# Norms begun in the block before: the head of a grouped attention and of a ternary MLP

## Chip, cores and metric

One core of one Trainium2 chip. The metric is the device time of one execution in microseconds, the median over several runs. In what follows TensorE is PE in the rows, VectorE is DVE, ScalarE is ACT, GpSimd is POOL.

## The reference

A decoder of four layers on x of shape (4, 256, 256), fp32. Each layer adds an attention, a cross attention and a feed-forward part, each on a layer norm of x:

```python
def _layernorm(x, axis=-1, eps=1e-05):
    m = jnp.mean(x, axis=axis, keepdims=True)
    v = jnp.var(x, axis=axis, keepdims=True)
    return (x - m) / jnp.sqrt(v + eps)
...
    x = x + _L1_ffn_ref(_layernorm(x, axis=-1), ...)
    x = x + _L2_attn_ref(_layernorm(x, axis=-1), L2_attn_wq, L2_attn_wk, L2_attn_wv, L2_attn_wo)
...
    x = x + _L3_xattn_ref(4, 256, 256, L3_xattn_w, L3_xattn_u, _layernorm(x, axis=-1), ctx_2048)
    x = x + _L3_ffn_ref(_layernorm(x, axis=-1), L3_ffn_W_up, L3_ffn_W_gate, L3_ffn_W_down)
```

Three parts matter here. `_L1_ffn_ref` is a mixture of 8 experts (top 2) with a narrow hidden size of 128, an up projection to 256 and a core product. `_L3_xattn_ref` is a recurrence over time (WKV) with keys from the norm and values from the context. `_L3_ffn_ref` is silu(x Wu') * (x Wg') Wd' with 1024 hidden columns and weights replaced by -1, 0 or 1 times a scale.

## The kernel before

The residual X lies in SBUF as 8 tiles of 128 tokens x 256, in four groups g of two tiles. The program is a row of blocks; within one, each engine has its own list of instructions, ordered by hand, with semaphores between them. At a block's end all engines meet in a barrier.

`norm_steps` (L273) gives the steps of a norm for one group. `measure` (VectorE): two statistics (L322), two aggregates (L325). `root` (ScalarE, L389): a square root, which needs a table of its own. `apply` (VectorE): a reciprocal (L329), two scalings (L332) into H. `turn` (TensorE): four transposes (L426) into a PSUM bank. `copy` (ScalarE): out of it, to HT (L394), or, where bf16 parts are wanted, to the first part (L396). Then `rest_of` (VectorE, L337) subtracts the first part, `second` (ScalarE, L400) rounds the rest, `third` (VectorE, L341) subtracts again: fp32 as a sum of three bf16 parts. `columns(g)` is the wait for the last of these. `warm` (L267) issues filler products of 512 columns, whose result is not used.

`experts1` (L2015) ends so: 42 pieces of up product, Gelu, gating and down product; the last down products; VectorE reads both PSUM banks (L2213) into MT; TensorE issues 8 up products (L2118) into banks 0 to 3, twice round; VectorE adds each to X (L2217). The next block, `project_paired` of layer 2 (L1225), runs the whole norm and the first projections: product and values (L1263, L1271) on TensorE, the rotation on VectorE (L1292 to L1296) and GpSimd (L1307), spread to masked copies on ScalarE (L1330).

`wkv_scan` (L2709) is the recurrence by scans. Its end: the last quotient (L2765), TensorE turns it onto X in PSUM (L2872, L2877), ScalarE copies the sum back to X (L2835), once for each of the four batches.

`ternary_mlp` (L2935) is the last block. It runs a norm with three parts from its first step on, then for 8 chunks i of the hidden columns and 2 halves c of the tokens: up and gate product (L2959, 12 matmuls), Silu (L2995), product with the gate (L3025), three parts (L3001, L3030, L3005, L3034), down product (L2969, 12 matmuls), with each up product one chunk ahead of the down product. At the end X gets the sum (L3049) and goes to DRAM.

TensorE's order at its head is

```python
                    warm(pe, 3, 8)
                    for g in range(TT // 2):
                        norm["turn"](pe, g)
                        warm(pe, 3, 4)
                    warm(pe, 3, 6)
                    for c in range(NCH):
                        go_up(0, c)
```

The first layer's `mlp` (L1532) is built alike, with groups 0 and 1 of its norm begun in the block before it, and turns only of groups 2 and 3 at its head.

## Time and profile before

| | |
|---|---|
| median of 3 runs | 1171.09 us (1167.62 to 1173.74) |
| the profiled execution | 1173.02 us |
| its span, first to last instruction | 1171.3 us |
| TensorE busy | 1058.0 us (90%) |
| VectorE busy | 778.7 us (66%) |
| ScalarE busy | 572.6 us (49%) |
| GpSimd busy | 384.9 us (33%) |
| mean granted TensorE clock | 0.968 of full |

The busy shares are averages over some thirty blocks with different limits; what a change in one place is worth is read in the timeline of that place. The profiled execution's time is its span and 1.7 us around it.

### The profile page before, as it was taken

The page shows a single profiled execution, that of the slowest core. Times are in us where ns is not written, and L with a number is a line of the kernel's source. Part 1 is how long each engine was busy: PE and PEld are TensorE (multiplying, and loading weights), DVE is VectorE, ACT ScalarE, POOL GpSimd, SP SyncE. Part 2 cuts the span into 40 slices and gives each one's busy share as a digit, 9 for nine tenths or more (in the row PEclk, how much of TensorE's full clock was granted, in tenths as well). Part 3 has the DMA queues.
Part 4 walks back from the last instruction along what each step waited for, and adds up shares of the span by engine and source line. Part 5 has one row for each costly group of instructions (what it writes and reads, how often), then busy time and mean ns, then how long its engine had stood idle before and what let it go on. Part 6 is the DMA issues. An engine that isn't in the chain of part 4 may idle for free. (4 is left out here: it accounts for less than half of the span.)

```text
span 1171.3 us, 22560 instructions
## 1 busy us (share of the span) xinstructions
PE 1058.0 (90%) x8162; PEld 657.3 (56%) x8177; DVE 778.7 (66%) x2357; ACT 572.6 (49%) x1193; POOL 384.9 (33%) x499
## 2 busy tenths in 40 slices
PE   5779989998989999899998989899999999867898
PEld 3447645567855554455665545467777555543455
DVE  6753468659668654567887678673454777969755
ACT  3859425564425624374555266516433154547443
POOL 2445403000001210033666425437776033843000
PEclk9889999998999999999999899999999999987999
DMA  9100000000031030000000000536665400000001
GB/s 376 59 1 3 1 1 2 1 1 2 1 157 79 2 144 1 0 1 3 2 3 2 1 2 2 194 109 206 187 193 151 144 1 2 2 1 0 1 1 37
DMA packets 23486, 60.74 MB, mean 52 GB/s; under 512 B 3681, under 2 KB 12009, under 8 KB 22480
## 3 DMA queue, kind: packets, MB, share of 16 engines
q1 hardware_dynamic: 18864, 48.92, 11.9%
q0 software_dynamic: 4512, 10.37, 3.0%
q8 instruction: 67, 1.10, 0.4%
q14 instruction: 43, 0.35, 0.1%
HBM read 52.95 MB, written 8.29 MB: 52 GB/s over the span
## 5 line engine op out<-in xcount | busy, mean ns | idle before, releaser
L977 ACT ACTIVATE PT<-PS 128x384 f32<-128x384 f32 (+1 forms) x320 | 153.2, 530 | 162.0 <-PE PS L721 115.9
L872 DVE CUSTOM_DVE_ANT_0 junk<-PS,TRI 128x128 bf16<-128x128 f32 (+1 forms) x384 | 111.0, 352 | 2.4 <-PE PS L702 2.4
L702 PE MATMUL PS<-KS,QM 32*128 32x128 f32 (+1 forms) x768 | 90.1, 344 | 8.7 <-ACT PT L977 1.6
L702 PEld LDWEIGHTS PS<-KS,QM 32*128 32x128 f32 x768 | 73.6, 184 | 41.2 <-issue 21.9
L270 PE MATMUL PS<-identb 128*128 128x512 bf16 x355 | 89.0, 390 | 3.7 <-PEq L481 1.1
L721 PE MATMUL PS<-QM,KS 32*128 32x256 f32 (+1 forms) x768 | 88.6, 348 | 0.5 <-ACT PT L977 0.2
L1058 POOL TENSOR_TENSOR OD<-OD 128x256 f32<-128x256 f32 x16 | 11.6, 728 | 226.7 <-DVE OD L932 226.7
L1036 POOL TENSOR_SCALAR_AFFINE_SELECT PT<-PT 128x512 f32<-128x512 f32 x96 | 60.4, 636 | 69.8 <-ACT PT L977 69.8
L791 PE MATMUL PS<-PT,VM 128*32 128x256 f32 (+1 forms) x1024 | 72.7, 359 | 8.5 <-POOL PT L1036 7.9
L1307 POOL TENSOR_TENSOR ROT<-RC,RS 128x512 f32<-128x512 f32 x16 | 20.3, 1270 | 148.6 <-DVE RS L1296 145.8
L721 PEld LDWEIGHTS PS<-QM,KS 32*128 32x128 f32 x768 | 65.8, 184 | 3.3 <-issue 2.7
L2393 PE MATMUL PS<-WU,XT 128*128 x188 | 63.6, 461 | 0.3 <-ACT XT L2487 0.3
L270 PEld LDWEIGHTS PS<-identb 128*128 128x128 bf16 x355 | 32.4, 99 | 46.2 <-issue 16.6
L2207 DVE SCALAR_TENSOR_TENSOR HB<-HA,ROW,GB 128x512 f32<-128x512 f32 x40 | 30.0, 751 | 39.6 <-ACT HA L2142 39.2
L2705 POOL DMA_INDIRECT chosen<-YB,DEST x47 | 48.1, 1022 | 18.8 <-issue 11.6
L2690 POOL DMA_INDIRECT XB<-token_rows,FROM x47 | 46.3, 985 | 20.7 <-issue 11.3
L2142 ACT ACTIVATE HA<-PS,VEC 128x512 f32<-128x512 f32 x42 | 28.7, 687 | 48.8 <-PE PS L2061 48.8
L2413 PE MATMUL PS<-WD,HIDT 128*128 128x256 f32 x188 | 48.2, 380 | 0.0
L426 PE MATMUL PS<-CST,H 128*128 128x128 f32 x128 | 23.3, 315 | 25.9 <-DVE H L332 25.6
L2553 DVE TENSOR_TENSOR HID<-PS,AE 128x176 f32<-128x176 f32 x47 | 16.0, 341 | 43.8 <-ACT AE L2493 43.7
L881 DVE TENSOR_REDUCE MA<-PS 128x4 f32<-128x1024 f32 x32 | 38.9, 1220 | 8.8 <-PE PS L702 7.6
L2061 PE MATMUL PS<-GH,WB 128*128 128x512 f32 x84 | 43.4, 599 | 0.6 <-ACT GH L2125 0.6
(399 smaller groups left out, 2649.2 us busy)
## 6 DMA issues: line engine op xcount, KB each, us to landing
WD<-w2d_in SPq DMA_DIRECT2D x47, 256.0 KB, 3.4
WU<-w2u_in SPq DMA_DIRECT2D x1, 5632.0 KB, 18.2
WA<-wl_in SPq DMA_DIRECT2D x1, 5137.0 KB, 16.1
GB<-gate_rows SPq DMA_DIRECT2D x8, 512.0 KB, 7.5
WU<-chosen SPq DMA_DIRECT2D x16, 256.0 KB, 5.7
WB<-wb_in SPq DMA_DIRECT2D x1, 3208.0 KB, 19.2
WA<-wa_in SPq DMA_DIRECT2D x1, 2560.0 KB, 16.0
WA<-w2s_in SPq DMA_DIRECT2D x6, 384.0 KB, 17.0
```

The lines of the kernel that those rows point to most:

```text
L270: pe.matmul(PS[:, bank, :].rearrange("p (a n) -> p a n", a=4), identb[:], identb[:].rearrange("p (a n) -> p a n", a=1).to_broadcast([P, 4, ...
L702: return pe.matmul(PS[:, s, m * T:m * T + n], queries(U, v)[rows, m * P:(m + 1) * P], keys(U, v)[rows, 0:n], start=True, stop=True, skip_g ...
L721: last = pe.matmul(bank, keys(U, v)[rows, n * P:(n + 1) * P], queries(U, v)[rows, lo:hi], start=n == 0, stop=r > 1, skip_group_check=True, ...
L791: last = pe.matmul(PS[at:at + 32, 7, side + lo:side + hi], VM[:, U % 2, n, h * P + at:h * P + at + 32], PT[:, g % 3, s, n * T:n * T + hi - ...
L872: last = dve.tensor_tensor_reduce(junk[:, s, m * P:m * T + P], PS[:, s, m * T:m * T + (m + 1) * P], TRI[:, (1 - m) * P:T], 1.0, NEG, ALU.a ...
L977: act.activation(PT[:, g % 3, st_slot(k), 0:W], PS[:, st_bank(g, k), 0:W], ACT.Exp, scale=scale).then_inc(S["at_exp"], 1)
L1036: pool.affine_select(v, v, [[0, 4], [1, P]], ALU.is_ge, 0.0, base=0, channel_multiplier=-1).then_inc(S["at_masked"], 1)
L2061: pe.matmul(PS[:, n % 2, :], w, GH[:, c * CH:(c + 1) * CH], start=True, stop=True).then_inc(S["up_ps"], 1)
L2393: last = pe.matmul(up_bank(b), XT[:, b % 2, k * P:(k + 1) * P], mine[:, k * 2 * I2:(k + 1) * 2 * I2], start=k == 0, stop=k == KD - 1)
L2413: last = pe.matmul(down_bank(b), HIDT[:, b % 2, k * P:(k + 1) * P], WD[:, b % RINGW, k * D:(k + 1) * D], start=k == 0, stop=k == 1)
L2690: pool.indirect_dma_start(XB[:, j, :], None, token_rows, bass.IndirectOffsetOnAxis(FROM[:, b:b + 1], 0)).then_inc(S[f"x_slot{j}"], 16)
L2705: pool.indirect_dma_start(chosen, bass.IndirectOffsetOnAxis(DEST[:, b:b + 1], 0), YB[:, b % RINGE, :], None, bounds_check=SPARE_ROW - 1, o ...
```

## The change

- The first norm of layer 2 is begun in `experts1`: VectorE measures and applies groups 0 and 1 there between the additions, ScalarE roots and copies them, TensorE turns them. The sum is read in two halves, and the last up products go to six banks instead of four. `project_paired` does only groups 2 and 3.
- The norm of the ternary MLP is begun in `wkv_scan`: measures and roots of groups 0 and 1 at the end of VectorE's and ScalarE's lists. `parts` moves to another place in SBUF's order of allocation.
- In `ternary_mlp` VectorE's and ScalarE's lists at the head are written out in a new order, with a Silu on one element ahead of the copies 2 and 3 (it brings the table) and the first Silu ahead of `second(3)`. TensorE's head is as before. The last chunk's down products go part by part.

```diff
@@ def experts1(norm, following):
+            following["begin"]()
+            last_bank = lambda t: PS[:, (0, 1, 2, 3, 6, 7, 0, 1)[t], 0:D]
...
-                    pe.wait_ge(S["dve_mark"], d["dve_mark"] + 3)
+                    pe.wait_ge(S["x_added"], d["x_added"] + TT // 2)
                     for t in range(TT):
-                        if t >= 4:
-                            pe.wait_ge(S["x_added"], d["x_added"] + TT // 2 + t - 3)
-                        pe.matmul(PS[:, t % 4, 0:D], MT[:, t * P:(t + 1) * P], wB("up"), start=True, stop=True
+                        if t % TPC == 0:
+                            pe.wait_ge(S["dve_mark"], d["dve_mark"] + 3 + t // TPC)
+                        if t >= 6:
+                            pe.wait_ge(S["x_added"], d["x_added"] + TT // 2 + t - 5)
+                        pe.matmul(last_bank(t), MT[:, t * P:(t + 1) * P], wB("up"), start=True, stop=True
                                   ).then_inc(S["o_proj"], 1)
+                    pe.wait_ge(S["x_added"], d["x_added"] + TT // 2 + 4)
+                    warm(pe, 2, 4)
+                    for g in range(BEGUN):
+                        following["turn"](pe, g)
+                        warm(pe, 2, 4)
...
+                    for g in range(BEGUN):
+                        following["root"](act, g)
+                    for g in range(BEGUN):
+                        following["copy"](act, g)
...
+                    for c in range(NCH):
+                        dve.wait_ge(S["down_ps"], d["down_ps"] + NWK - NCH + c + 1)
+                        dve.tensor_scalar(MT[:, c * CH:(c + 1) * CH], PS[:, 4 + c, :], cc[:, 2:3], None, ALU.add
+                                          ).then_inc(S["dve_mark"], 1)
+                    for g in range(BEGUN):
+                        add_last(2 * g)
+                        add_last(2 * g + 1)
+                        dve.wait_ge(S["x_added"], d["x_added"] + TT // 2 + 2 * g + 2)
+                        following["measure"](dve, g)
+                    for g in range(BEGUN):
+                        following["apply"](dve, g)
+                    for t in range(2 * BEGUN, TT):
+                        add_last(t)
@@ def wkv_scan(left, norm, following):
                     quotients(B - 1)
+                    for g in range(BEGUN):
+                        dve.wait_ge(S["x_added"], d["x_added"] + g + 1)
+                        following["measure"](dve, g)
...
                     for b in range(1, B):
                         copy(b)
+                    for g in range(BEGUN):
+                        following["root"](act, g)
@@ def ternary_mlp(exact, SC, norm):
+                    def last_down(c):
+                        for j, name in enumerate(("pr_first", "pr_second", "pr_third")):
+                            pe.wait_ge(S[name], d[name] + NCH * (n - 1) + c + 1)
+                            for q in range(TPC):
+                                last = down_step(n - 1, c, q, j)
+                        last.then_inc(S["down_ps"], 1)
...
-                    norm["scalar"](act)
...
+                    norm["copy"](act, 0)
+                    norm["copy"](act, 1)
+                    norm["second"](act, 0)
+                    norm["root"](act, 2)
+                    norm["second"](act, 1)
+                    norm["root"](act, 3)
+                    act.activation(AO[:, 0, 0:1], SC[:, 0:1], ACT.Silu)
+                    norm["copy"](act, 2)
+                    norm["copy"](act, 3)
+                    norm["second"](act, 2)
                     silu(*work[0])
+                    norm["second"](act, 3)
...
-                    norm["vector"](dve)
+                    for g in range(BEGUN):
+                        norm["apply"](dve, g)
+                    norm["measure"](dve, 2)
+                    norm["rest_of"](dve, 0)
+                    norm["rest_of"](dve, 1)
+                    norm["third"](dve, 0)
+                    norm["measure"](dve, 3)
+                    norm["third"](dve, 1)
+                    norm["apply"](dve, 2)
+                    norm["apply"](dve, 3)
+                    for g in (2, 3):
+                        norm["rest_of"](dve, g)
+                    for g in (2, 3):
+                        norm["third"](dve, g)
```

VectorE at the end of `experts1`, in the changed program (L2235 reads the sum, L2231 is an addition to X, L322 to L332 are the norm's):

```order
L2235 TENSOR_SCALAR MT<-PS,cc 128x512 [waits down_ps] x2
L2231 TENSOR_TENSOR X<-X,PS 128x256 [waits o_proj] x2
L322 BN_STATS HEAD_STATS<-X 128x6 [waits x_added]
L322 BN_STATS HEAD_STATS<-X 128x6
L325 BN_AGGR HEAD_MOM<-HEAD_STATS 128x2 [waits stats] x2
L2231 TENSOR_TENSOR X<-X,PS 128x256 [waits o_proj] x2
L322 BN_STATS HEAD_STATS<-X 128x6 [waits x_added]
L322 BN_STATS HEAD_STATS<-X 128x6
L325 BN_AGGR HEAD_MOM<-HEAD_STATS 128x2 [waits stats] x2
L329 RECIPROCAL HEAD_RSTD<-HEAD_STD 128x2 [waits std]
L332 TENSOR_SCALAR H<-X,HEAD_MOM,HEAD_RSTD 128x256 [waits rstd]
L332 TENSOR_SCALAR H<-X,HEAD_MOM,HEAD_RSTD 128x256
```

Before, the reading was one instruction and the eight additions stood in one piece, with the block's end behind them; the norm's rows stood in the next block.

ScalarE from the last copies of the recurrence into the ternary MLP, before and now (L2835 and L2865 are the copies of X, L389 the root, L396 the first part, L400 the second part, L2995 and L3035 the Silu):

```order
L2835 ACTIVATE X<-PS 128x512 [waits turned] x3
L2727 UNCONDITIONAL_BRANCH
L2987 UNCONDITIONAL_BRANCH [waits barrier_Pool_Activation_PE_DVE_SP_release]
L389 ACT_TABLE_LOAD
L389 ACTIVATE std<-mom,CST 128x2 [waits moments] x3
L396 ACTIVATE parts<-PS 128x2x256 [waits turned]
L389 ACTIVATE std<-mom,CST 128x2 [waits moments]
```

```order
L2865 ACTIVATE X<-PS 128x512 [waits turned] x3
L389 ACT_TABLE_LOAD
L389 ACTIVATE HEAD_STD<-HEAD_MOM,CST 128x2 [waits moments] x2
L2754 UNCONDITIONAL_BRANCH
L3029 UNCONDITIONAL_BRANCH [waits barrier_Pool_Activation_PE_DVE_SP_release]
L396 ACTIVATE parts<-PS 128x2x256 [waits turned] x2
L400 ACTIVATE parts<-HT 128x2x256 [waits part_rest]
L389 ACTIVATE HEAD_STD<-HEAD_MOM,CST 128x2 [waits moments]
...
L400 ACTIVATE parts<-HT 128x2x256 [waits part_rest]
L3035 ACTIVATE AO<-PS,SC 128x512 [waits up_ps]
L400 ACTIVATE parts<-HT 128x2x256 [waits part_rest]
```

The table load and two roots moved from behind the branch, which is the block's end, to ahead of it; the first Silu stands ahead of the last L400.

VectorE at the head of the ternary MLP, in the changed program:

```order
L322 BN_STATS HEAD_STATS<-X 128x6 x2
L325 BN_AGGR HEAD_MOM<-HEAD_STATS 128x2 [waits stats] x2
L337 TENSOR_TENSOR HT<-PS,parts 128x2x256 [waits part_first] x2
L341 TENSOR_TENSOR parts<-HT,parts 128x2x256 [waits part_second]
L322 BN_STATS HEAD_STATS<-X 128x6 x2
L325 BN_AGGR HEAD_MOM<-HEAD_STATS 128x2 [waits stats] x2
L341 TENSOR_TENSOR parts<-HT,parts 128x2x256 [waits part_second]
L329 RECIPROCAL HEAD_RSTD<-HEAD_STD 128x2 [waits std]
L332 TENSOR_SCALAR H<-X,HEAD_MOM,HEAD_RSTD 128x256 [waits rstd]
L332 TENSOR_SCALAR H<-X,HEAD_MOM,HEAD_RSTD 128x256
```

Before, `measure` and `apply` of all four groups (L322 to L332) stood ahead of the first L341; now the scalings of groups 2 and 3 stand behind the L341 of groups 0 and 1, while TensorE's list still has its turns of groups 2 and 3 ahead of the first up product.

## Rows read from the trace of the kernel before

**Rows 1.** Chain of waits that ended last: start us, us, what.
```profile
1102.90 7.72 PE PS L2959 x35
...
1158.73 2.60 PE PS L2959 x12
...
1161.35 0.70 ACT AO L2995
```

**Rows 2.** Timeline, end of the experts: start us, us, engine, line, what [idle before it <- releaser].
```profile
485.24 2.85 PE L2067 MATMUL PS<-HB,WB 128*128 128x512 f32 x6
...
489.47 3.72 PE L2118 MATMUL PS<-WB,MT 128*128 128x256 f32 x16 [1.38 <-DVE MT L2213]
490.21 3.44 DVE L2217 TENSOR_TENSOR X<-X,PS 128x256 f32<-128x256 f32 x8 [0.79 <-PE PS L2118]
...
500.06 1.98 PE L1263 MATMUL PS<-HT,WA 128*128 128x512 f32 x4 [0.39 <-ACT HT L394]
...
502.09 0.73 DVE L1292 STREAM_SHUFFLE RS<-PS 128x512 f32<-128x512 f32 x1
...
504.13 1.26 POOL L1307 TENSOR_TENSOR ROT<-RC,RS 128x512 f32<-128x512 f32 x1 [90.31 <-DVE RS L1296]
...
507.16 2.55 ACT L1330 ACTIVATE QM<-ROT,CST 128x512 f32<-128x512 f32 x4
```

**Rows 3.** Timeline, end of the recurrence and head of the ternary MLP.
```profile
1089.66 0.69 DVE L2765 TENSOR_TENSOR EV<-PS,EV 128x512 f32<-128x512 f32 x1
...
1091.60 0.60 ACT L2835 ACTIVATE X<-PS 128x512 f32<-128x512 f32 x1 [2.30 <-PE PS L2877]
1092.45 1.28 ACT L389 ACT_TABLE_LOAD   x1 [0.26 <-PEq L2727]
...
1092.49 1.89 PE L270 MATMUL PS<-identb 128*128 128x512 bf16 x8 [0.93 <-PEq L2727]
...
1093.75 0.29 ACT L389 ACTIVATE std<-mom,CST 128x2 f32<-128x2 f32 x1
...
1094.23 0.13 DVE L329 RECIPROCAL rstd<-std 128x2 f32<-128x2 f32 x1
...
1110.45 1.47 PE L2969 MATMUL PS<-WA,MP 128*128 128x256 bf16 x12
```

**Rows 4.** Groups by line, 1092.4 to 1103.6 us: xcount | busy us, mean ns | idle.
```profile
L322 DVE BATCH_NORM_STATS2 stats<-X 128x6 f32<-128x256 f32 x8 | 3.0, 412 | 2.1 <-PEq L2727 2.1
L332 DVE TENSOR_SCALAR H<-X,mom,rstd 128x256 f32<-128x256 f32 x8 | 2.9, 410 | 0.1
...
L337 DVE TENSOR_TENSOR HT<-PS,parts 128x512 f32<-128x512 f32 x4 | 2.7, 683 | 0.0
L426 PE MATMUL PS<-CST,H 128*128 128x128 f32 x16 | 2.6, 287 | 1.2 <-DVE H L332 1.2
L400 ACT ACTIVATE parts<-HT 128x512 bf16<-128x512 f32 x4 | 2.5, 626 | 0.8 <-DVE HT L337 0.8
L396 ACT ACTIVATE parts<-PS 128x512 bf16<-128x512 f32 x4 | 2.3, 587 | 1.1 <-PE PS L426 1.1
```

**Rows 5.** Windows: length, PE, PEld, DVE, ACT, POOL busy (instructions), granted clock, DMA share, GB/s.
```profile
1072.60:1075.29 2.69, 0.01 (x1) 0.00 (x1) 2.69 (x6) 2.65 (x7) 0.00 (x0) 0.92 0.00 0
1075.29:1078.00 2.71, 2.71 (x3) 1.17 (x4) 2.71 (x1) 2.71 (x8) 2.63 (x3) 0.50 0.00 0
...
674.48:676.73 2.25, 0.00 (x1) 0.03 (x1) 1.55 (x3) 2.22 (x4) 0.00 (x0) 1.00 0.00 0
676.73:678.73 2.00, 2.00 (x20) 1.05 (x20) 0.83 (x1) 1.16 (x3) 0.00 (x0) 1.00 0.00 0
1047.60:1064.40 16.80, 7.52 (x17) 4.00 (x18) 15.60 (x31) 14.64 (x32) 1.40 (x1) 0.50 0.00 0
```

**Rows 6.** Timeline, head of the first layer's MLP.
```profile
216.62 0.69 ACT L1622 ACTIVATE AO<-PS,VEC 128x512 f32<-128x512 f32 x1 [0.83 <-PE PS L1553]
...
218.60 0.98 PEld L1553 LDWEIGHTS PS<-QT,WA 128*128 128x128 bf16 x6 [0.94 <-DVE QT L341]
```

**Rows 7.** Timeline, the last products and additions.
```profile
1165.52 1.40 DVE L3049 SCALAR_TENSOR_TENSOR X<-PS,SC,X 128x512 f32<-128x512 f32 x2
...
1165.65 1.48 PE L2969 MATMUL PS<-WA,MP 128*128 128x256 bf16 x12 [0.69 <-DVE MP L3034]
...
1167.18 1.41 DVE L3049 SCALAR_TENSOR_TENSOR X<-PS,SC,X 128x512 f32<-128x512 f32 x2 [0.26 <-PE PS L2969]
```

More of the change, by code:

```diff
@@ L432, in tensor @@
                 turn(pe, g)
-        return dict(rest_of=rest_of, parts=parts, vector_rest=vector_rest, scalar_rest=scalar_rest, begin=begin, root=root, copy=copy, measure=measure, apply=apply, vector=vector, scalar=scalar, tensor=tensor, product=product, turn=turn, columns=columns, tokens=tokens)
+        return dict(rest_of=rest_of, third=third, second=second, parts=parts, vector_rest=vector_rest, scalar_rest=scalar_rest, begin=begin, root=root, copy=copy, measure=measure, apply=apply, vector=vector, scalar=scalar, tensor=tensor, product=product, turn=turn, columns=columns, tokens=tokens)
     def add_sums(gate=None):
@@ L2012, in mixing, with experts1 @@
             done["moments"] += 3 * TT
-    def experts1(norm):
+    def experts1(norm, following):
         E = E1
@@ L2720, in wkv_scan @@
             done["dve_chain"] += 5
+            done["turned"] += B
+            done["x_added"] += B
+            following["begin"]()
             K = HT[:].rearrange("p k (b t) -> p k b t", t=T)
@@ L2886, in _ @@
                     turn(B - 1)
-            done["turned"] += B
-        left.close()
     def ternary():
@@ L2945, in ternary_mlp @@
             MP = tmp("MP3", [P, 3, NCH, CH], BF16)
-            norm = norm_steps(st, X, H, to_HT, parts=parts, tbank=lambda g: 4 + g)
+            parts = norm["parts"]
             d = dict(done)
@@ L2980, in _ @@
                         go_up(0, c)
-                    for i in range(n):
+                    for i in range(n - 1):
                         for c in range(NCH):
-                            if i + 1 < n:
-                                go_up(i + 1, c)
+                            go_up(i + 1, c)
                             go_down(i, c)
+                    for c in range(NCH):
+                        last_down(c)
                 @block.scalar
                 def _(act):
-                    norm["scalar"](act)
                     def silu(i, c):
@@ L3104, in layers @@
         cross_attention(32, gamma=rv("gamma"), loads=late_loads, following=following)
-        experts1(following)
+        first = norm_steps(None, X, H, to_HT, tbank=lambda g: 4 + g, begun=False)
+        experts1(following, first)
         wb_store.close()
@@ L3114, in layers @@
                                   "v": wL("v3", KD), "o": wL("o3", KD)}, 16, 0.25, turned=True, begun=second)
-        wkv_scan(left, norm)
-        parts = sb("parts", [P, 3, KD, B * T], BF16)
-        ternary_mlp(exact, SC, parts)
+        parts = left.enter_context(nc.sbuf_tensor("parts", [P, 3, KD, B * T], BF16))
+        last = norm_steps(None, X, H, to_HT, parts=parts, tbank=lambda g: 4 + g, begun=False)
+        wkv_scan(left, norm, last)
+        ternary_mlp(exact, SC, last)
+        left.close()
     layers()
```

34 lines of the change are left out of this document (17 added, 17 removed).

## The prediction

> **What bounds the kernel now.** The chain of waits says where the end is set: from 1102.9 us to 1161 us it is TensorE alone, the ternary MLP's up and down products back to back [rows 1]. What moves their start moves the end of the program by the same amount. So I read the timeline at the three places that the change touches: the end of the first expert stage [rows 2], the end of the recurrence and the head of the ternary MLP [rows 3], and the last products [rows 7]. The groups by line give the norm steps' durations [rows 4]. The first layer's MLP, whose order is copied, shows how that order behaves [rows 6], and the windows show TensorE's granted clock around its pauses [rows 5]. At all three places work is serial: TensorE waits for a norm, and nothing else fills the time.
>
> **Place 1, end of the experts to the first projection.** Before: the last down products end at 488.09, TensorE stands for 1.38 us until VectorE has read both halves of the sum in one step, the eight up products run from 489.47, eight additions from 490.21 take 3.44 us, and the next block's first projection starts at 500.06 [rows 2]. Now:
> - The sum is read in two halves. The first is complete before the last down product's end and hides beside it, so the up products start at about 488.0. The second half, some 0.7 us (half of the 1.38), is done by 488.8, before the fifth product asks for it.
> - VectorE: two additions from 488.75 (0.43 each), measure of group 0 (two statistics and two aggregates; two measures lie between 1092.49 and 1094.23 [rows 3], so 0.88 us), two additions, measure of group 1, apply 0, apply 1 (two scalings of 0.41 us each [rows 4], the reciprocal ahead in their overlap: 0.82), and four additions. 488.75 + 4 x 0.43 + 2 x 0.88 + 2 x 0.82 + 4 x 0.43, with 0.1 us of waits on its own results, is 495.7.
> - TensorE turns group 0 when it is applied, at 493.2, and group 1 after four filler products of 0.22 us, at 494.6; the last four fillers are out at 495.95. ScalarE has been idle since the last Gelu, so the table load for the root hides there.
> - With 0.3 us between blocks the first projection starts at 496.3 instead of 500.06: **-3.8 us**. VectorE still has measures and applies 2 and 3 ahead of the first rotation (496.35 + 2 x 0.88 + 2 x 0.82 = 499.75), which before began at 502.09: 2.3 us earlier rather than 3.8, so 1.5 us are missing. The cover is ScalarE's order: it copies groups 2 and 3 before the first values and the first spread, which before began at 507.16, 1.77 us after GpSimd's sum of the rotation was ready (504.13 + 1.26) [rows 2]. 1.5 is less than 1.77, so the spread still comes 3.8 us earlier and the gain passes on; if that cover were gone, 1.5 us would be given back. The projection now carries the wait for the late weights that the fillers carried; those were issued without standing, so it costs nothing.
>
> **Place 2, recurrence to ternary MLP.** The measures of groups 0 and 1 go behind the last quotient on VectorE, which ends at 1090.35, so they are over by 1092.1 and cost nothing. But the two roots stand behind ScalarE's last copy of X, which ends at 1092.20, and need another table: a load of 1.28 us and two roots of 0.29 us, 1094.0, and all engines wait for it in the block's barrier. The new block starts at 1094.3 instead of 1092.5 [rows 3]. Before, the first reciprocal ran at 1094.23 [rows 3]; so beginning the norm early gains nothing for group 0.
>
> From 1094.3 on, with the new order on VectorE and ScalarE and the same one on TensorE (all four turns stand ahead of the first up product):
> - TensorE's eight fillers end at 1096.03, later than group 0 is applied (1095.24). Turn 0 at 1096.03, turn 1 behind it and four fillers at 1097.38, ending 1098.04 (four transposes, 0.66 us from the first start to the last end: 0.29 of [rows 4] for one, three issues of 0.12).
> - VectorE: applies 0 and 1, measure 2, rest 0 and 1 (each behind ScalarE's 0.59 us copy), third 0, measure 3, third 1, over at 1101.5, each tensor step 0.68 us. Only then apply 2, done at 1102.3, and apply 3 at 1103.1.
> - TensorE, idle from 1098.7, turns group 2 at 1102.34, group 3 at 1103.70, issues ten fillers and starts the first up product at 1106.35, against 1102.90 [rows 1]: +3.5 us.
> - The second half's up product needs third 3. ScalarE now takes the first Silu (0.70 us [rows 1], behind the first up product's end at 1108.94) ahead of second 3 (0.63), and third 3 (0.68) follows [rows 4]: 1110.95. TensorE stands for 2.0 us. The first layer's MLP shows just this: a Gelu at 216.62, its next up product only at 218.60 [rows 6]. Before, that product started right behind the first.
> - Two up products of 2.6 us later [rows 1], the first down product starts at 1116.13; before it was 1110.45 [rows 3]. That is **+5.7 us**, and everything behind is bound by TensorE, so it stays.
>
> **TensorE's clock at place 2.** TensorE now rests twice: from its last turn's end, just before ScalarE's copy of 1091.60 [rows 3], to 1094.3 (2.7 us), and from 1098.7 to 1102.34 (3.6 us). In the row of 1072.60, a pause of 2.69 us from the full 2.4 GHz, the granted clock falls (its mean over the pause is 0.92), and it is 0.50 (1.2 GHz) all through the next 2.71 us: with the pause's end over 3 us at half clock, I take 3.3 [rows 5]. Of five such pauses of 2.69 to 2.87 us in this trace at full clock all five are followed by half clock; one of 2.25 us is not [rows 5]. While TensorE is the one that is waited for, a stretch of 3.3 us at half clock does half its work: 1.7 us lost. Unknown is how much of each stretch falls on work that matters. The lower bound is 0 (the 2.25 us row); the upper is three such stretches, about 5 us, as the level may stay low: it did for 16.8 us from 1047.6, where TensorE was busy for 7.52 [rows 5]. I take two stretches, **+3.4 us**, since both pauses are at or over the length that always fell.
>
> **Place 3, the end.** The last piece's products are issued part by part, so only four products of 0.12 us (1.48 / 12 [rows 7]) wait for the last third, at 1165.65: TensorE would end near 1166.2 instead of 1167.13. But VectorE's first two additions run until 1166.92 anyway, and its idle time before the third was 0.26 us [rows 7]. So **-0.3 us**; the other 0.7 us hide behind VectorE.
>
> **Sum:** -3.8 + 5.7 + 3.4 - 0.3 = **+5.0 us**. The profiled execution took 1173.02 us, 1.7 us more than its span and 1.9 us more than the median of the three runs, 1171.09. That one would become 1178.0; the median, which I predict, **1176.1 us**. A measurement of this kernel can tell 0.5% from no change, 5.9 us; the forecast is just under it.
>
> **A rule against the sum.** The roots' table load costs 1.28 us in the trace: the load of 1092.45 ends at 1093.73 and the root stands at 1093.75, with nothing between [rows 3]. The Trainium skill, "ScalarE: Activation LUTs", section "What ACT_TABLE_LOAD costs", adds a drain of about 1380 ns to every switch. By that the block would start about 1.4 us later, and the sum would be an estimated +6.4 us. The trace has the load alone, so I keep 1.28 and give the drain the small chance below.
>
> **Rivals.**
> - *The clock holds.* A pause that shares its time with much activity around it may pass, as at 674.48. Then the sum is -3.8 + 5.7 - 0.3 = +1.6 us, 1172.7. For it: fillers surround both pauses. Against: five of five. 0.15.
> - *The low clock stays longer, slower than before.* Mechanism: with half clock already at 1094.3 the eight fillers take 3.5 us, both turns and with them copy, rest and third of groups 0 and 1 come 1.7 to 2.5 us later, the pause behind them follows at half clock, and the 2.0 us wait for the first Silu meets it while it is still low, and it stays low beyond. It decides once the clock is down before the first filler. Price: +5.7 + 5 or more, so the sum is +7 to +9: 1178 to 1180. For it: the long low stretch from 1047.6. 0.24.
> - *ScalarE stands some more than its load at the recurrence's end,* 1.4 us, before the barrier lets the block begin. The same load at a block's head shows nothing of the kind [rows 3]. +6.4, 1177.5: 0.03.
> - *Place 1 gives nothing*, because VectorE's later rotation or a lost cover takes its gain: -3.8 becomes -1: +7.8, 1178.9. 0.05.
> - *Faster.* Stretches at half clock lie elsewhere too, and all stages behind place 1 move by 3.8 us, which may shorten or lengthen them. The one from 1047.6 to 1064.4 held 7.5 us of TensorE work [rows 5]; at full clock that is 3.8 us less. With that, and the clock holding at place 2, it is -2; to be faster by 5.9 a second such one must vanish. 0.08.
> - *Forecast as it stands,* +2.5 to +7: 0.45.
>
> **How the numbers follow.** Of the forecast's 0.45, some 0.32 lie under 5.9 us and 0.13 over. Within 0.5%: 0.32 + 0.15 = 0.47, and 0.01 from place 1. Slower: 0.13 + 0.24 + 0.03 + 0.04 = 0.44. Faster: 0.08. The range for 8 in 10 goes from below the case in which the clock holds, 1170.5, to the longer low clock, 1181; the forecast's own is 1173.6 to 1178.1.
>
> **What would show it.** Right: the first projection starts 3.8 us after the place where the down products end plus 4.5 us, that is some 8.3 us behind them instead of 12; a table load with two roots between ScalarE's last copy of the recurrence and the new block; turn 2 waiting some 3.6 us for the apply; the second up product waiting about 2 us behind a Silu; the granted clock at 0.5 around there. Wrong: if from the last quotient to the first ternary down product it is not at least 25 us (before: 1110.45 - 1090.35 = 20.1), the step on the order at place 2 falls; if it is about 26 with the clock at 1.0, only the clock's term falls.

## Result and the profile after

| | before | after |
|---|---|---|
| median, 10 executions each | 1172.09 us (1167.44 to 1175.90) | 1177.24 us (1171.85 to 1181.85) |
| the profiled execution | 1173.02 us | 1176.54 us |
| its span | 1171.3 us | 1174.8 us |
| mean granted TensorE clock in it | 0.968 | 0.966 |

The ratio is 1.0046, with [1.0028, 1.0064] as its 95% interval: by it the change is 5.4 us slower (3.3 to 7.5); the two medians differ by 5.15 us. The forecast was +5.0. The two profiled executions differ by 3.5 us. The difference between these two numbers is a question of its own, and the experiments come to it.

**Place 1.** Timeline of the changed kernel, from the last down products of the experts into the next block: start us, us, engine, line, what [idle before it <- releaser].

```profile
484.80 2.85 PE L2073 MATMUL PS<-HB,WB 128*128 128x512 f32 x6
...
485.71 1.28 ACT L389 ACT_TABLE_LOAD   x1
...
487.62 3.69 PE L2126 MATMUL PS<-WB,MT 128*128 128x256 f32 x16
487.69 0.75 DVE L2235 TENSOR_SCALAR MT<-PS,cc 128x512 f32<-128x512 f32 x1 [0.23 <-PE PS L2073]
...
492.70 0.66 PE L426 MATMUL PS<-CST,H 128*128 128x128 f32 x4 [0.53 <-DVE H L332]
...
495.96 1.96 PE L1263 MATMUL PS<-HT,WA 128*128 128x512 f32 x4 [0.45 <-PEq L2048]
...
499.22 0.73 DVE L1292 STREAM_SHUFFLE RS<-PS 128x512 f32<-128x512 f32 x1
...
501.27 1.28 POOL L1307 TENSOR_TENSOR ROT<-RC,RS 128x512 f32<-128x512 f32 x1 [87.89 <-DVE RS L1296]
...
503.03 2.55 ACT L1330 ACTIVATE QM<-ROT,CST 128x512 f32<-128x512 f32 x4
```

The down products end at 484.80 + 2.85 = 487.65. The up products start at that moment, without the pause of 1.38 us [rows 2], and the first projection starts 8.31 us behind the end, not 11.97 (500.06 - 488.09 [rows 2]): -3.66 us. The table load at 485.71 lies beside the down products. The program is 0.44 us ahead already before this place (487.65 against 488.09), which is not the change's. Net of it, VectorE's rotation starts 2.43 us earlier, and the spread (L1330) 3.69 us earlier. So the gain passes on whole, although VectorE's share of it is smaller.

**Place 2.** Timeline of the changed kernel, same columns, from the last quotient to the first ternary down product.

```profile
1085.94 0.69 DVE L2792 TENSOR_TENSOR EV<-PS,EV 128x512 f32<-128x512 f32 x1
...
1086.68 1.16 PE L2910 MATMUL PS<-CST,EV 128*128 128x128 f32 x8 [0.88 <-DVE EV L2792]
...
1087.88 0.60 ACT L2865 ACTIVATE X<-PS 128x512 f32<-128x512 f32 x1 [2.31 <-PE PS L2910]
...
1088.49 1.28 ACT L389 ACT_TABLE_LOAD   x1
1089.79 0.48 ACT L389 ACTIVATE HEAD_STD<-HEAD_MOM,CST 128x2 f32<-128x2 f32 x2
...
1090.58 2.66 PE L270 MATMUL PS<-identb 128*128 128x512 bf16 x8 [2.73 <-PEq L2754]
...
1093.03 1.06 PE L426 MATMUL PS<-CST,H 128*128 128x128 f32 x4
...
1100.19 0.66 PE L426 MATMUL PS<-CST,H 128*128 128x128 f32 x4 [3.45 <-DVE H L332]
...
1104.14 2.75 PE L2990 MATMUL PS<-parts,WA 128*128 128x512 bf16 x12
1106.94 0.69 ACT L3035 ACTIVATE AO<-PS,SC 128x512 f32<-128x512 f32 x1 [3.63 <-PE PS L2990]
1107.52 0.62 ACT L400 ACTIVATE parts<-HT 128x512 bf16<-128x512 f32 x1
...
1108.92 5.35 PE L2990 MATMUL PS<-parts,WA 128*128 128x512 bf16 x24 [2.02 <-DVE parts L341]
...
1114.11 1.47 PE L3011 MATMUL PS<-WA,MP 128*128 128x256 bf16 x12
```

From the last quotient's start to the first down product it was 1110.45 - 1089.66 = 20.79 us [rows 3]; it is 1114.11 - 1085.94 = 28.17: +7.38 us. Each wait that the order promised is there: 2.73 us of TensorE behind the table load and the roots, 3.45 us for the applied group 2, and 2.02 us for the last part, which stands behind the Silu.

The chain of waits of the changed kernel says why the second wait is there: start us, us, what.

```profile
1096.55 0.69 DVE HT L337
1097.23 0.60 DVE parts L341
1097.84 0.66 DVE HEAD_STATS L322 x2
1098.50 0.22 DVE HEAD_MOM L325 x2
1098.71 0.57 DVE parts L341
1099.29 0.09 DVE HEAD_RSTD L329
...
1099.40 0.75 DVE H L332 x2
```

It runs through VectorE without a hole: the third parts of groups 0 and 1 (L341) and a measure stand ahead of group 2's apply (L332). The two L341 are parts for an up product that TensorE's list does not let run before turns 2 and 3.

TensorE's clock in windows of the changed kernel, around its pauses: length, PE, PEld, DVE, ACT, POOL busy (instructions), granted clock, DMA share, GB/s.

```profile
1087.84:1090.58 2.74, 0.01 (x1) 0.04 (x2) 0.52 (x4) 2.36 (x4) 0.00 (x0) 1.00 0.00 0
...
1091.60:1095.00 3.40, 3.40 (x11) 1.75 (x10) 1.86 (x7) 0.60 (x1) 0.00 (x0) 0.51 0.00 0
...
1096.74:1100.19 3.45, 0.00 (x1) 0.00 (x0) 3.41 (x11) 2.52 (x5) 0.00 (x0) 1.00 0.00 0
1100.20:1103.60 3.40, 3.40 (x20) 2.12 (x21) 2.22 (x6) 2.06 (x5) 0.00 (x0) 1.00 0.03 5
```

The pause behind the recurrence was followed by half clock (1.2 GHz): the eight fillers took 2.66 us instead of 1.89 [rows 3], and turn 0 took 1.06 instead of 0.66. The longer pause of 3.45 us was not; here the clock stayed at 2.4 GHz. The three other traces with this head (`e2`, `e4` and `e11` below) show the same: half clock behind the first pause, full clock behind the second.

**Place 3.** Timeline of the changed kernel, its last products and additions, same columns as above.

```profile
1168.59 1.34 PE L3011 MATMUL PS<-WA,MP 128*128 128x256 bf16 x8 [0.40 <-ACT MP L3045]
1169.18 2.72 DVE L3113 SCALAR_TENSOR_TENSOR X<-PS,SC,X 128x512 f32<-128x512 f32 x4
```

The four additions run through where there was a hole of 0.26 us between them [rows 7]. From the first down product to the last addition's end it is 57.79 us instead of 58.14: -0.35.

The three add up to -3.66 + 7.38 - 0.35 = +3.4 us for the profiled execution, which is its difference of 3.5.

### The profile page after: what moved, and what is told of

The parts are those of the page before. It is cut to its first block and busy times, and to the rows that moved or that the text cites. A ratio compares the mean times of both kernels' runs of the same rounds, so it can differ in the third digit from the quotient of the medians.

```text
span 1174.8 us, 22573 instructions
## 1 busy us (share of the span) xinstructions
PE 1059.0 (90%) x8174; PEld 658.2 (56%) x8174; DVE 778.6 (66%) x2358; ACT 572.7 (49%) x1194; POOL 384.5 (33%) x499
## 5 line engine op out<-in xcount | busy, mean ns | idle before, releaser
L2714 POOL DMA_INDIRECT XB<-token_rows,FROM x47 | 46.0, 980 | 20.7 <-issue 10.7
L426 PE MATMUL PS<-CST,H 128*128 128x128 f32 x128 | 23.5, 317 | 27.7 <-DVE H L332 27.5
L2990 PE MATMUL PS<-parts,WA 128*128 128x512 bf16 x192 | 43.9, 379 | 2.0 <-DVE parts L341 2.0
```

The costliest lines, as they stand in the source:

```text
L2714: pool.indirect_dma_start(XB[:, j, :], None, token_rows, bass.IndirectOffsetOnAxis(FROM[:, b:b + 1], 0)).then_inc(S[f"x_slot{j}"], 16)
L2990: last = pe.matmul(PS[:, 2 * c + half, :], w[:, k, i * P:(i + 1) * P], parts[:, j, k, c * CH:(c + 1) * CH], start=k == 0 and j == 0, stop= ...
```

## Experiments

Twelve runs were made in three groups of four, each group on a chip of its own beside the kernel before: `e1` to `e4` (before: median 1199.93 us), `e5` and `e7` to `e9` (1201.76), `e6` and `e10` to `e12` (1175.01). They are eleven programs, the change itself among them; one was run twice. "Q" below is the start of the recurrence's last quotient, and "to down" the time from there to the first ternary down product: 20.79 us before, 28.17 in the change. On the first two of these chips the whole program takes some 25 us longer than on the third, nearly all of it in the second expert stage between places 1 and 2, where nothing was changed; the stretches at the three places are the same to 0.1 us. So the stretches are compared across chips, and the times only as ratios.

### Which part costs: the parts alone

`e1_place1_alone` has the change's `experts1` and `project_paired`, and the recurrence and `ternary_mlp` of before. `e2_places23_alone` is the reverse:

```diff
-        first = norm_steps(None, X, H, to_HT, tbank=lambda g: 4 + g, begun=False)
-        experts1(following, first)
+        experts1(following)
```

> Place 1 alone (the norm of layer 2 begun in the experts' tail), recurrence and ternary MLP as before. My theory: the first projection starts about 8 us behind the last down product instead of 12, and the last quotient of the recurrence is reached 3.7 us earlier; nothing after it changes, so the kernel is 3.7 us faster than before, ratio 0.997. Rival (the gain is given back on the way, or by stretches at half clock that fall elsewhere): the ratio is 1.000 or above.

Measured: ratio 0.9977 [0.9956, 0.9997]; the first projection 8.31 us behind the down products, to down 20.79. The rival's 1.000 lies just outside the interval.

> Places 2 and 3 alone, the experts as before. My theory: from the start of the last quotient (20.8 us before the first down product of the ternary MLP in the kernel before) it takes 26.5 us with the clock up and 28.2 with one stretch at half clock; the end gives 0.35 back; so +6 to +8 us, ratio 1.005 to 1.007. Rival (the loss comes from how the two parts meet, for instance the clock's phase that place 1 shifts): less than +4 us.

Measured: 1.0053 [1.0033, 1.0073]; 11.97 us to the first projection, to down 28.17. The stretches are additive to the hundredth: place 1 gains 3.66 us, place 2 loses 7.38, and neither changes the other.

### The clock: filling the pauses

`e3_pause_filled` puts twelve fillers behind the recurrence's last turn, for the first pause:

```diff
+                    warm(pe, 0, 12)
```

> The changed kernel with 12 filler products behind TensorE's last turn of the recurrence, which fill the 2.7 us pause until the new block. Clock theory: the granted clock stays at 1.0 at the head of the ternary MLP, the first turn ends 0.9 us or more earlier, and from the last quotient's start to the first down product it takes 26.5 us instead of 28.2. Rival (order and barrier alone cost the 7.4 us, and half clock hides beside the waits for VectorE): still 28 us. A second risk: the fillers end late and delay the block's start; 12 x 0.216 = 2.6 us from 1087.8 is just inside the pause.

Measured: 1.0021 [1.0004, 1.0038]; to down 30.01. TensorE's timeline in this run:

```profile
1114.46 2.75 PE L270 MATMUL PS<-identb 128*128 128x512 bf16 x12
1117.51 1.89 PE L270 MATMUL PS<-identb 128*128 128x512 bf16 x8 [0.30 <-PEq L2754]
...
1125.45 0.65 PE L426 MATMUL PS<-CST,H 128*128 128x128 f32 x4 [3.45 <-DVE H L332]
1125.94 1.42 PE L270 MATMUL PS<-identb 128*128 128x512 bf16 x4
...
1135.86 7.04 PE L2991 MATMUL PS<-parts,WA 128*128 128x512 bf16 x24 [2.02 <-DVE parts L341]
```

The first pause is gone, and the eight fillers take 1.89 us again. But now the clock fell in the second pause and once more behind the third, where 24 up matmuls took 7.04 us instead of 5.35. Turn 0 ended about 1 us earlier, as expected, but 30.01 is neither the theory's 26.5 nor the rival's 28: in this execution the fall came where it cost more. The second risk that was named came true in small: the fillers end late, and the block begins at Q + 4.79 instead of Q + 4.64.

`e9_both_pauses_filled` has those twelve and nineteen fillers behind turn 1:

```diff
-                        warm(pe, 3, 4)
+                        warm(pe, 3, 19 if g == 1 else 4)
```

> The changed kernel with 12 fillers behind the recurrence's last turn and 19 instead of 4 behind turn 1, so that TensorE works through both pauses. Clock theory: granted clock 1.0 up to the first up product, which starts 16.7 us behind the last quotient (18.2 in the changed kernel, 18.4 with the first pause alone filled), and the first down product at 26.5 us. Only the 2.0 us pause behind the first up product can still lower it. Rival (half clock is not what these 1.7 us are): 28 us.

Measured: 1.0032 [1.0011, 1.0053]; to down 26.64, and the window shows the full clock all through the head (same columns as the windows above):

```profile
1115.00:1139.40 24.40, 21.81 (x107) 10.47 (x107) 13.41 (x35) 11.77 (x21) 0.00 (x0) 1.00 0.00 1
```

So with the clock up place 2, new order and table load together, costs 26.64 - 20.79 = +5.85 us. What the clock took in the profiled execution of the change is 28.17 - 26.64 = 1.53 us, and in the run with one pause filled 30.01 - 26.64 = 3.37. Here too the twelve fillers put the block 0.15 us late (Q + 4.79), and turn 2 comes as much later, 7.94 us behind the block's start. Without that the price is an estimated +5.70 and the clock's part 1.68; the figures below use 5.85 and 1.53. The rival that half clock is not what these 1.7 us are falls (28 us), and so does the idea that the clock explains most of place 2.

### The order: taking back one step at a time

`e4_silu_behind_second` moves the first Silu behind the spread of group 3:

```diff
-                    silu(*work[0])
                     norm["second"](act, 3)
+                    silu(*work[0])
```

> The changed kernel with the first Silu put back behind second(3) on ScalarE. My theory: the 2.0 us in which TensorE stood before the second up product vanish, the two first up products run back to back, and from the last quotient's start to the first down product it takes 26.2 us (28.2 less 2.0). Rival (the Silu ahead saves as much later as it costs, as the first down product's chain starts from it): 27.5 us or more.

Measured: 1.0018 [0.9998, 1.0038]; to down 25.97 instead of 28.17. The two up products run as one group again, 7.93 us without a hole. The Silu's place is worth 2.2 us of the 5.85; the rival (27.5 us or more) falls.

`e5_table_early` loads the root's table ahead of ScalarE's last copy of X, by a root of a constant that nothing reads:

```diff
+                        if b == B - 1:
+                            act.activation(nsq[:], cst("eps"), ACT.Sqrt)
```

> The changed kernel with one square root on a single element ahead of ScalarE's last copy of X in the recurrence, so that the table is loaded in ScalarE's idle time. My theory: the load was on the path to the barrier; the new block's first filler starts 3.35 us behind the last quotient's start instead of 4.64, TensorE's pause there falls from 2.7 to 1.4 us, and the first down product comes 25.2 us behind the last quotient with the clock up (28.2 in the changed kernel), 26.9 or more if the clock falls in the second pause. Rival (the copy of X cannot run with the square root's table and another load follows, or the measures on VectorE set the block's end): 27.8 us or more.

Measured: 1.0050 [1.0017, 1.0082], 7 executions; to down 28.44. ScalarE and TensorE in its timeline:

```profile
1113.62 1.28 ACT L2881 ACT_TABLE_LOAD   x1
...
1114.91 0.20 ACT L2881 ACTIVATE nsq<-CST 128x1 f32<-128x1 f32 x1
...
1116.14 0.47 ACT L389 ACTIVATE HEAD_STD<-HEAD_MOM,CST 128x2 f32<-128x2 f32 x2
1116.92 1.89 PE L270 MATMUL PS<-identb 128*128 128x512 bf16 x8 [1.31 <-PEq L2755]
```

The block begins 1116.92 - 1113.71 = 3.21 us behind Q instead of 1090.58 - 1085.94 = 4.64: the load's 1.43 us are gone from the path. The last copy of X (1115.65 to 1116.25) and the two roots follow without a second load. But the clock fell behind the second pause and again behind the third as in `e3_pause_filled` (24 up matmuls took 7.04 us), so the gain does not show in the end: 28.44 lies in the range of the rival, but neither of the rival's two reasons is in the trace.

`e6_up_first` lets TensorE issue the first half's up product ahead of turns 2 and 3 and drops six fillers:

```diff
-                    warm(pe, 3, 6)
-                    for c in range(NCH):
-                        go_up(0, c)
+                        if g == 1:
+                            go_up(0, 0)
+                    go_up(0, 1)
```

> Edit, from the change: the first half of unit 0's up product stands ahead of the projections of tiles 2 and 3, the second half behind them, and the six fillers between go. Theory A (the second pause in the head is the time in which the first half's product and everything behind it could run, and the order of TensorE keeps them out): first up product at about 12 us behind the last quotient's start (18.20 in the change), the second half still waits for tiles 2 and 3, first down product at about 24.8 with the clock up (28.17 in the change), so about 3.4 us less than the change: ratio 1.000. Rival B (the parts of the second half bound the head alone): first up product early, but first down product at 27 or later and less than 1.2 us gained: ratio 1.002 to 1.005. Rival C: the clock falls behind the wait for tiles 2 and 3, which would put 1.5 to 3.4 us back on A, first down product at 26.3 to 28.2.

Measured: 0.9992 [0.9969, 1.0014]; first up product at Q + 13.65, to down 26.14. The clock was at half from 1087.4 to 1091.0, on the same eight fillers as in the change. So against the change's 28.17 TensorE's list alone was worth 2.0 us; the six fillers that were dropped had no part in it, since TensorE stood for 2.17 us behind the last filler even so. Theory A's 24.8 and its first up product at 12 are for the clock up. The stretch at half clock is the change's own (turn 1 starts at Q + 9.35, there Q + 9.34, with both pauses filled Q + 7.82 with the fillers' 0.15 in it). With its estimated 1.68 us taken off, 26.14 becomes 24.5 and 13.65 becomes 12.0: theory A holds, and of its 3.4 us against the change 2.0 are order and the rest is clock. Rival B (27 us or more) falls. Rival C's condition, a fall behind the wait for groups 2 and 3, did not come.

### Can the early norms pay

`e8_head_mended` combines the early table, TensorE's up product between the turns and the Silu behind the spread; it also moves `third(1)` ahead of `measure(3)` and has other numbers of fillers:

```diff
                     norm["turn"](pe, 1)
+                    warm(pe, 3, 9)
+                    go_up(0, 0)
                     norm["turn"](pe, 2)
...
+                        act.activation(nsq[:], cst("eps"), ACT.Sqrt)
...
-                    silu(*work[0])
                     norm["second"](act, 3)
+                    silu(*work[0])
```

> The changed kernel with place 2 mended: table loaded early, the first up product ahead of turns 2 and 3 and in their pause, thirds 0 and 1 ahead of measure 3, first Silu behind second(3), fillers 5, 2, 9 and 8. My theory: no pause of TensorE over 1.5 us but at the barrier, granted clock 1.0, first down product 20.7 us behind the last quotient's start, as in the kernel before (20.8): beginning the norm early is worth nothing there even when its costs are taken away, since ScalarE's copy and the barrier take the place of the first measures. Ratio 0.9965. Rival (the early measures were a gain that the order alone spoilt): 19.5 us or less.

Measured: 0.9986 [0.9965, 1.0007]; first up product at Q + 10.47, to down 22.04. That is 1.3 us over the expected 20.7, since the clock fell here, behind a pause of only 1.31 us:

```profile
1122.18 2.06 PE L270 MATMUL PS<-identb 128*128 128x512 bf16 x5 [1.31 <-PEq L2755]
1124.03 1.06 PE L426 MATMUL PS<-CST,H 128*128 128x128 f32 x4
```

`e10_interleaved`, the next kernel, has the same list on TensorE up to this point and the same pause of 1.31 us, and there the clock did not fall:

```profile
1089.27 1.24 PE L270 MATMUL PS<-identb 128*128 128x512 bf16 x5 [1.31 <-PEq L2755]
1090.35 0.60 PE L426 MATMUL PS<-CST,H 128*128 128x128 f32 x4
```

It puts the turns, copies, rests, spreads and parts of the four groups in the order in which they come ready, with the early table. ScalarE's list, for example:

```diff
+                    norm["root"](act, 2)
                     norm["copy"](act, 0)
                     norm["copy"](act, 1)
-                    norm["second"](act, 0)
-                    norm["root"](act, 2)
-                    norm["second"](act, 1)
                     norm["root"](act, 3)
-                    act.activation(AO[:, 0, 0:1], SC[:, 0:1], ACT.Silu)
+                    norm["second"](act, 0)
                     norm["copy"](act, 2)
+                    norm["second"](act, 1)
```

> Edit, from the change: the square root's table is loaded ahead of the recurrence's last output copy (as in the run with the early table), TensorE's projections of the four tiles stand in the order in which their parts come (five fillers, tile 0, two, tile 1, three, tile 2, three, tile 3, three, then both halves of the up product), ScalarE and VectorE alternate between the tiles in the same order, and the Silu of unit 0 goes behind the spread of tile 3. Theory A (what lengthened the head is the order and the table load, each of which can be taken back while the two norms stay ahead): first ternary down product 19.2 us behind the start of the last quotient (20.79 before, 28.17 in the change, 22.04 in the mended head), first up product at 11.4; with places 1 and 3 the sum is -3.7 -0.35 -1.6 = -5.6 us, ratio 0.995. Rival B (a stretch at half clock falls into it, as it did in the mended head at 22.04): 1.5 to 3.4 us more, first down product at 20.7 to 22.6, ratio 0.997 to 0.998. Rival C (beginning the norms early gives nothing that the order of before does not give): first down product at 20.8 or later with the clock up, and the time that of places 1 and 3 alone, 0.9947 to 0.997.

Measured: 0.9951 [0.9927, 0.9975]; first up product at Q + 12.59, to down 20.14, with one stretch at half clock while TensorE turned groups 2 and 3:

```profile
1095.00:1098.40 3.40, 3.34 (x11) 1.46 (x10) 2.73 (x7) 1.95 (x4) 0.00 (x0) 0.52 0.02 5
```

That is 0.65 us under the order of before even so: rival C, that nothing is to be gained on the order of before, is refuted in the trace, and B's mechanism probably took part of the 1.6 us. That the 0.65 us come from the early norms, and not from the new order and the fewer fillers, is not shown: an interleaved order without early norms was not run.

`e7_places13` keeps places 1 and 3 and leaves place 2 as it was, and `e12_places13_again` is the same program. Added to place 1 alone is only the end:

```diff
-                    for i in range(n):
+                    for i in range(n - 1):
...
+                    for c in range(NCH):
+                        last_down(c)
```

> Places 1 and 3 only: the norm of layer 2 begun in the experts' tail, the last down products part by part; recurrence and head of the ternary MLP as before. My theory: 8.3 us from the last down product of the experts to the projection, 20.8 us from the last quotient to the first down product, 57.8 us from there to the last addition: -3.7 and -0.35, ratio 0.9966 to before. Rival (the end's gain needs the new head): 58.1 us for the last stretch.

> Places 1 and 3 without place 2, once more with more rounds, since the single measurement gave 0.9947 [0.9926, 0.9968] where the two stretches alone add up to -3.66 -0.35 = -4.0 us (0.9967), and place 1 alone gave 0.9977. Theory A (the gain is the two stretches and no more): 0.9955 to 0.998, first down product 20.8 us behind the last quotient's start. Rival B (something between the two places gains as well): 0.994 to 0.995 again.

Measured: 0.9947 [0.9926, 0.9968] and 0.9938 [0.9915, 0.9960]; the stretches 8.31, 20.79 and 57.79 us both times, so the end's gain does not need the new head. It beats both kernels: 1168.72 us beside 1175.01 for before on the same chip, and 1179.51 for the change. The interleaved head had 1169.00 there, which is no difference. Both ratios lie below theory A's 0.9955 to 0.998, where rival B had put them. Part of what is over the -4.0 us goes with a higher clock, as the table below shows; for the rest rival B, a gain somewhere between the two places, is not excluded.

### The change once more, and where the spread lies

> The change itself, on the chip of these runs, so that the others are compared with it beside the same runs of the kernel before. Theory A (the change costs what its stretches cost: -3.7 at the experts' start, +7.4 at the ternary head with one stretch at half clock, -0.35 at the end): +3.4 us, ratio 1.003; with a second stretch at half clock, as where one pause had been filled, up to +5.3, ratio 1.0045. Rival B (the change costs something outside these three stretches too): 1.005 or more with the stretches as they were. First down product 28.2 us behind the last quotient's start by A, 30.0 where a second stretch at half clock falls into the head.

Measured: 1.0045 [1.0026, 1.0064], 1179.51 us; to down 28.18, one stretch at half clock. The profiled execution, 1175.33, was the second fastest of the twelve. The stretches give +3.4, the ratio +5.3. The ratio is that of theory A with two stretches at half clock, but the trace shows one. Each execution comes with its mean granted clock, though. Three of the twelve of the change and three of the 27 of before on this chip, chosen along the range:

| | clock, time | clock, time | clock, time |
|---|---|---|---|
| before | 0.972, 1168.69 us | 0.967, 1171.95 | 0.964, 1175.63 |
| change | 0.967, 1175.33 us | 0.963, 1178.09 | 0.960, 1181.52 |

A straight line with one slope for all five kernels of a chip gives 0.90 us less for each 0.001 of clock on the last chip (+- 0.09; each +- here is a 95% interval), 0.78 and 0.77 on the other two; around it the executions scatter by 1.0 to 1.7 us. For the 27 of before on the last chip the standard deviation is 2.8 us as measured and 0.9 around a line of their own. So most of the spread from run to run goes with the time at half clock; that one causes the other is argued, not shown. The line parts the cost in two: the difference at equal clock, and the difference in clock.

| kernel | executions | at equal clock, us | stretches with the clock up, us | its mean clock less before's |
|---|---|---|---|---|
| place 1 alone | 12 | -3.6 +- 0.9 | -3.7 | -0.0008 |
| places 2, 3 alone | 7 | +5.5 +- 1.1 | +5.5 | -0.0008 |
| one pause filled | 10 | +2.1 +- 1.0 | +1.8 | -0.0010 |
| both filled | 10 | +2.3 +- 1.3 | +1.8 | -0.0017 |
| Silu behind second | 10 | -0.6 +- 1.0 | -0.4 | -0.0026 |
| early table | 7 | +2.5 +- 1.5 | +0.3 | -0.0040 |
| head mended | 12 | -3.3 +- 1.2 | | -0.0029 |
| up first | 10 | -0.6 +- 0.7 | | 0.0000 |
| interleaved | 8 | -6.6 +- 0.8 | | -0.0013 |
| places 1, 3 | 8 and 8 | -3.3 +- 1.4, -4.9 +- 0.8 | -4.0 | +0.0023, +0.0007 |
| the change | 12 | +2.1 +- 0.8 | +1.8 | -0.0035 |

The fourth column is -3.66, then what "to down" has over 20.79 with the clock's 1.53 or 3.37 us taken off, then -0.35 (place 1 alone: the first; "Silu behind second": 25.97 - 1.53; early table: 28.44 - 3.37); it is empty where the clock's share was not measured apart. Nine times the equal clock can be held against the stretches. Seven agree; the second run of places 1 and 3 is just outside (-4.9 + 0.8 = -4.1), and the early table, with seven executions, is 2.2 us off for a reason that stays open. The change's clock is 0.0035 lower (0.9628 against 0.9663, standard errors 0.0007 and 0.0005), and 3.5 x 0.90 is 3.1 us: +2.1 and +3.1 are the +5.2 by which its mean execution is slower. That the lower clock comes from place 2 is likely and not shown: of the nine kernels with groups begun in the recurrence eight have a lower mean clock than before (-0.0008 to -0.0040) and one the same, and the two runs without it but with place 3 have a higher one. On the chip of `e1` to `e4`, places 2 and 3 alone lowered it by only 0.0008, with standard errors of 0.0006 and 0.0005. Where in those other executions the half clock lies was not seen, since only one of each kernel has a trace. The interleaved head is 1.8 +- 1.0 us ahead of places 1 and 3 at equal clock, near the 1.6 us expected of it, but its clock is 0.0020 lower, and in the medians nothing is left of the gain.

## Why the prediction was right

The total, 1176.1 us against 1177.24, and the sign of the probable difference were right. The forecast started from a median of three, 1171.09, where ten gave 1172.09; the difference, +5.0 against +5.15, was closer still. Its steps of order and waits are each found in the traces. That the total is so close is partly luck, for it rests on the clock's term, a choice between 0 and 5 us whose reason the traces contradict. By its steps:

- **Place 1:** -3.8 forecast, -3.66 measured. The projection "some 8.3 us behind" is at 8.31. The cover that was named for VectorE's later rotation held: rotation 2.4 us earlier (2.3 forecast), spread 3.69 us earlier. The rival that place 1 gives nothing is refuted by its run alone.
- **The table load between the last copy and the block:** there at 1088.49, 1.28 us, with the roots at 1089.79. It is 0.01 us behind the copy's end and the root 0.02 us behind its own, so ScalarE stood for no drain. The Trainium skill, "ScalarE: Activation LUTs", section "What ACT_TABLE_LOAD costs", puts a drain of about 1380 ns beside the load at every switch; this case's trace doesn't agree. Loading early gave back 1.43 us, of which 1.28 is the load: the rest of 0.15 leaves no room for such a drain either.
- **The order at place 2:** +5.7 forecast, +5.85 with the clock up, of which 0.15 is the test fillers' own. Turn 2 waited 3.45 us (3.6), the second up product 2.02 us (2.0), the first up product came 16.89 - 13.24 = 3.65 us later (3.5), again with those 0.15. The test named for it, at least 25 us from the quotient's end, reads 28.17 - 0.69 = 27.5, and "about 26 with the clock at 1.0" is what both pauses filled gave, 25.95.
- **TensorE's clock:** +3.4 forecast. In the profiled execution it took 1.53 (1.68 without the test fillers' delay): this term was mis-sized there, and the step that failed is "I take two stretches ... since both pauses are at or over the length that always fell". Behind the first pause the clock fell; behind the second, 3.45 us long, it stayed at 1.0, in all four traces with this head. Over the executions of the last chip the lower clock is worth 3.1 us, near the forecast, but as a mean over executions that differ, not as two stretches in each. That it fell behind the second pause once the first was filled (`e3`) or cut to 1.31 us (`e5`) shows that the length of the pause before it does not decide alone. The trace of before held a sign of that, which the count of "five of five" left out: ahead of the long stretch at half clock from 1047.6 lies a pause of only 1.98 us, shorter than the one of 2.25 us that passed (same columns as the windows above):

```profile
1044.48:1046.46 1.98, 0.00 (x1) 0.00 (x1) 1.24 (x10) 0.29 (x1) 0.00 (x0) 1.00 0.04 8
...
1047.60:1050.00 2.40, 1.12 (x4) 0.72 (x4) 2.36 (x8) 0.44 (x2) 0.00 (x0) 0.50 0.00 0
```

- **Place 3:** -0.3 forecast, -0.35 measured.
- **The rivals:** "the clock holds" (+1.6) is near what equal clock gives, +2.1 +- 0.8, but in no trace of the change did the clock hold in the head. "The low clock stays longer" did not come in a trace of the change; the slowest executions cost as much as its +7 to +9, and where their half clock lies is not known. Slower by over 0.5% had 0.44, within 0.5% had 0.48: the ratio of 1.0046 lies just inside, and its interval holds the bound.

## What to carry to other kernels

A norm begun early can lose if not every engine's list is changed with it. At place 2 VectorE prepared the first half's parts ahead of the second half's apply, while TensorE's list still had the second half's turns ahead of the first product, so each engine waited for work that the other had put last; the same idea with the lists in agreement was 0.65 us ahead of before in the trace. In the medians it gave no more than leaving place 2 alone (1169.00 and 1168.72 us), which was 0.6% faster than before. Ask of a step moved across a barrier what it needs on its engine, as a table, and whether that is loaded beside other work (place 1, free) or in front of everyone (place 2, 1.43 us). And where a clock changes, compare executions at equal mean clock: this parted a difference of 5.2 us into 2.1 of work and waits at the three places and 3.1 that go with the clock, which neither the median nor one trace shows.

## What the runs showed of the hardware

- Whether the granted clock falls to half behind a given pause depends on more than that pause: behind 2.74 us it fell and behind 3.45 us it did not in four traces, and behind 3.45 us it fell in the two where the earlier pause was filled or cut short. Behind the same pause of 1.31 us, after the same work of TensorE in the head, it fell in the mended head and not in the interleaved one. Filling one pause is therefore no sure gain (28.17 us without, 30.01 with it). What decides was not tried apart.
- The same program differs by some 25 us between chips, nearly all in one stage. The second expert stage ran from 793.9 to 932.2 us in `e8`, and from 793.4 to 905.5 us in the trace of before, on another chip, for the same 47 blocks. TensorE was busy for all 119.00 us from 790 us on in before and for 131.23 of 145.00 in `e8`, at a granted clock of 1.00 and 0.93. What differs was not looked into.
- On one chip the executions of one program spread over 9 us, 1168.06 to 1176.87, and their mean clock goes with it, 0.972 to 0.962.
